# Where the keys and values of a second attention are projected: two other stages take them over

## The reference

```
x = x + decay_attention(layernorm(x))                       # L0_attn
x = x + causal_attention(layernorm(x), ctx, ctx)            # L0_xattn, bf16 projections
x = x + experts(layernorm(x))                               # L0_ffn: 8 experts, the best 2 for each token
x = x + rwkv_time_and_channel_mix(layernorm(x))             # L1_attn
x = x + biased_attention(layernorm(x), ctx, ctx, bias)      # L1_xattn
x = x + float8_ffn(x normalised)                            # L1_ffn
```

```
Q = query @ Wq.T + bq;  K = ctx @ Wk.T + bk;  V = ctx @ Wv.T + bv          # 16 heads of 16
scores = Q K^T / sqrt(16) + lambda_bias * bias ;  out = softmax(scores) V ;  out @ Wo.T + bo
```

## Time and profile before

| | us |
|---|---|
| median of 3 runs | 1992.35 (1987.86 to 1992.54) |
| profiled execution | 1993.02 |
| its span | 1991.2 |
| TensorE busy | 1691.7 (85%) |
| VectorE busy | 1248.1 (63%) |
| ScalarE busy | 1103.6 (55%) |
| GpSimd busy | 566.1 (28%) |
| granted TensorE clock, mean | 0.942 of full |

### The profile page before, as it was taken

One profiled execution on the slowest core, in us unless ns is written; L12 is line 12 of the kernel. 1 busy time (PEld: TensorE's weight loads), 2 busy tenths in 40 slices (PEclk: granted clock), 3 DMA queues, 4 the chain that ended last, 5 costly groups with the idle time before them and its releaser, 6 DMA issues. The chain is left out here.

```text
span 1991.2 us, 40593 instructions
## 1 busy us (share of the span) xinstructions
PE 1691.7 (85%) x13412; PEld 1393.7 (70%) x13412; DVE 1248.1 (63%) x4276; ACT 1103.6 (55%) x2520; POOL 566.1 (28%) x719
## 2 busy tenths in 40 slices
PE   6577777774899999999956999999988999999963
PEld 5455555553688888889944877787766888888842
DVE  6689999858211111111118999999936988888856
ACT  2299999920222222223325666666636888888845
POOL 3433233230211111101025566666520000000017
PEclk9899999976899999999977999999998999999975
DMA  3100010025455555558930000000001000000002
GB/s 117 47 26 25 19 26 18 2 80 183 135 180 187 181 186 183 185 174 267 323 129 14 19 22 22 22 22 22 12 12 40 23 23 23 23 23 23 2 1 85
DMA packets 102046, 154.64 MB, mean 78 GB/s; under 512 B 5760, under 2 KB 85504, under 8 KB 101088
## 3 DMA queue, kind: packets, MB, share of 16 engines
q1 hardware_dynamic: 85600, 125.25, 19.1%
q0 software_dynamic: 6480, 17.70, 3.0%
q10 hardware_dynamic: 9776, 9.31, 1.3%
HBM read 134.54 MB, written 17.69 MB: 76 GB/s over the span
## 5 line engine op out<-in xcount | busy, mean ns | idle before, releaser
L1836 ACT ACTIVATE moe_hT<-moe_p_h,lane_a 128x256 f32<-128x256 f32 (+1 forms) x344 | 131.4, 433 | 370.3 <-PE moe_p_h L1788 370.0
L1788 PE MATMUL moe_p_h<-moe_gT,moe_w 128*128 128x256 f32 (+1 forms) x1376 | 256.1, 345 | 0.8 <-issue 0.8
L1330 ACT ACTIVATE xb_pr<-xb_sc,xb_nmax 128x256 f32<-128x256 f32 x512 | 225.5, 502 | 50.7 <-DVE xb_nmax L1407 50.6
L1798 PE MATMUL moe_p_y<-moe_w,moe_hT 128*128 128x256 f32 x1136 | 252.3, 379 | 0.0
L1788 PEld LDWEIGHTS moe_p_h<-moe_gT,moe_w 128*128 128x128 f32 x1376 | 227.6, 192 | 25.7 <-issue 1.2
L1798 PEld LDWEIGHTS moe_p_y<-moe_w,moe_hT 128*128 128x128 f32 x1136 | 212.5, 190 | 27.1
L1407 DVE CUSTOM_DVE_ANT_0 xb_sc<-xb_p_s,xb_neg 128x256 f32<-128x256 f32 x512 | 187.0, 420 | 47.2 <-PE xb_p_s L1182 43.7
L837 ACT ACTIVATE xa_pr<-xa_sc,xa_nmax 128x256 f32<-128x256 f32 (+1 forms) x512 | 204.0, 453 | 17.6 <-DVE xa_nmax L917 17.2
L1705 POOL DMA_INDIRECT moe_gx<-moe_tokens,moe_source_i x71 | 67.4, 949 | 457.2 <-PE moe_p_t L1775 400.6
L1956 DVE COPY moe_gT<-moe_p_t 128x512 f32<-128x512 f32 (+1 forms) x43 | 25.7, 599 | 232.3 <-PE moe_p_t L1775 232.3
L1981 DVE TENSOR_TENSOR moe_gy<-moe_p_y,lane_a 128x256 f32<-128x256 f32 x71 | 27.5, 421 | 229.1 <-PE moe_p_y L1798 229.1
(11 more groups left out here) (331 smaller groups left out, 3454.3 us busy)
## 6 DMA issues: line engine op xcount, KB each, us to landing
moe_w<-in_L_ffn_w_dram SPq DMA_DIRECT2D x86, 1024.0 KB
moe_rows_out<-moe_gy ACTq DMA_DIRECT2D x28, 256.0 KB
X<-in_x_dram SPq DMA_DIRECT2D x4, 1024.0 KB, 10.9
xa_ctx<-in_ctx_turned_dram SPq DMA_DIRECT2D x16, 256.0 KB, 2.8
moe_tokens<-moe_XN_s SPq DMA_DIRECT2D x16, 256.0 KB, 2.1
xb_ctx<-in_ctx_turned_dram SPq DMA_DIRECT2D x16, 256.0 KB
xb_raw<-in_fside_BxSxS_dram SPq DMA_DIRECT2D x16, 256.0 KB
out_dram<-X SPq DMA_DIRECT2D x2, 1280.0 KB, 5.2
```

The costliest lines, as they stand in the source:

```text
L1330: last = act.activation(pr[:, n % RB, e, :], sc[:, n % RB, e, :], ACT.Exp, bias=nmax[:, n % RB, e:e + 1], scale=-1.0)
L1788: last = pe.matmul(p_h[n % 3][:, k * width:(k + 1) * width], w1[:, r, ic, (2 * n + k) * P:(2 * n + k + 1) * P], gT[:, r % 2, ic, 0:width], ...
L1798: last = pe.matmul(p_y[:, t * D:(t + 1) * D], hT[:, hc, t * P:(t + 1) * P], w2[:, r, hc, :], start=(hc == 0), stop=(hc == HC - 1))
L1836: last = act.activation(hT[:, 2 * n + k, 0:width], p_h[n % 3][:, k * width:(k + 1) * width], ACT.Gelu, bias=b1[:, bass.ds(e * HC + 2 * n + ...
```

## The change

Keys and values of the second attention are projected in `experts_ffn` (the first 18 units, `EARLY`) and in `time_channel_mix` (the other 14, `LATE`). Here a unit is one batch's keys or one batch's values: unit 2n is the keys of batch n, 2n+1 its values. They are stored to DRAM (`kv_all`) without their biases. `biased_attention` loads them, and GpSimd adds the biases.

In `experts_ffn` the weights and a ring of four contexts lie in slot 3 of the weights' ring and the results wait for their stores in slot 2, so the experts' weights for blocks 2 and 3 are loaded only when all stores have landed:

```diff
+            for u in range(3):
+                project_context(u)
             pe.wait_ge(s_["both_ready"], 1)
...
             pe.matmul(p_t[:, 0:NT * E], ones[:, :], both_v, start=True, stop=True).then_inc(s_["counted"], 1)
+            for u in range(3, 9):
+                project_context(u)
             for g in range(2 * NT // 8):
...
                 last.then_inc(s_["hot_read"], 1)
+                if g < 7:
+                    project_context(9 + g)
+            for u in range(16, EARLY):
+                project_context(u)
```

A unit is four products (`project_context`), into one of two new banks:

```diff
+            def project_context(u):
+                n, m = divmod(u, 2)
+                if u == 0:
+                    pe.wait_ge(s_["wkv_in"], 16)
+                if m == 0:
+                    pe.wait_ge(cx_in[n % 4], 16 * (n // 4) + 16)
+                if u >= 2:
+                    pe.wait_ge(s_["kv_read"], u - 1)
+                for k in range(DC):
+                    for ic in range(DC):
+                        if m == 0:
+                            last = pe.matmul(p_kv[m][:, k * S:(k + 1) * S], w_kv[:, 0, ic, k * P:(k + 1) * P], cx[:, n % 4, ic, :],
+                                             start=(ic == 0), stop=(ic == DC - 1))
...
+            def read_kv(u):
+                act.wait_ge(s_["kv_proj"], u + 1)
+                if u >= 8:
+                    act.wait_ge(kept_kv[u % 8], 16 * (u // 8))
+                act.activation(held[u % 8], p_kv[u % 2][:, :], ACT.Copy).then_inc(s_["kv_read"], 1)
```

ScalarE reads units 0 to 2 ahead of its two exponentials and the rest behind them. SP loads the weights at batch 6 of the first part and four contexts at batches 8 to 11, and then:

```diff
+            for u in range(4):
+                store_kv(u)
             sp.wait_ge(s_["owned"], 1)
             for j, r, i in groups(sp):
+                if isinstance(j, int) and j == 1:
+                    for u in range(4, 12):
+                        store_kv(u)
+                if isinstance(j, int) and j == 2:
+                    for u in range(12, EARLY):
+                        store_kv(u)
+                    for n in range(8):
+                        sp.wait_ge(kept_kv[n], 16 * ((EARLY - n + 7) // 8))
+                    sp.wait_ge(s_["kv_proj"], EARLY)
```

`store_kv(u)` waits for the read of unit u, and after an odd u it loads the context four further on. In `time_channel_mix` the same functions use `lane_a` for the weights, hid_sq for the contexts, hid for the results (a ring of four) and four banks:

```diff
+            for u in range(6):
+                project_context(u)
             turn_x(0, None)
+            project_context(6)
             for m in range(3):
                 project(0, m)
+            for u in range(7, 11):
+                project_context(u)
             pe.wait_ge(s_["xa_ready"], 1)
             turn_x(1, None)
+            for u in range(11, LATE):
+                project_context(u)
+            pe.wait_ge(s_["kv_read"], LATE)
```

In `biased_attention` the four functions of the keys and values go from TensorE's and VectorE's lists, GpSimd gets them, and the steps are ordered anew:

```diff
+            def finish_keys(n, h, s):
+                wait_alone(pool, s_["stood_p"], (kv_in[s], 32 * h + 32))
+                if since(n, 1):
+                    wait_alone(pool, s_["stood_p"], (s_["scored"], UNITS * (n - 1)))
+                for c in range(DC):
+                    last = pool.tensor_scalar(k[:, s, c, :], k_in[:, s, c, :], cols[:, 1, c:c + 1], None, ALU.add)
+                last.then_inc(s_["k_ready"], 1)
...
             for b, h, s in long_turns(pool, drain=2):
                 if since(b, 2):
                     add(b - 2)
+                if has_next(b):
+                    finish_keys(b + 1, h + s, 1 - s)
+                    finish_values(b + 1, 1 - s)
...
                 for g in range(STEPS if not at(b, B + 1) else 1):
+                    m = unit_before(b, g, 1)
+                    if m is not None:
+                        turn_unit(b, m)
+                        turn_unit(b, m + 1)
                     if runs(b):
                         scores(b, s, g)
...
-                    m = unit_before(b, g, 1)
                     if m is not None:
-                        turn_unit(b, m)
-                        turn_unit(b, m + 1)
+                        turn_unit(b, m + 2)
+                        turn_unit(b, m + 3)
                     if g == 0 and since(b, 2):
                         pe.wait_ge(s_["oT_ready"], b - 1)
                         project_rows(oT, 3, s_["y_ready"])
```

201 lines of the change are left out of this document (127 added, 74 removed).

## The result

The changed kernel takes 1969.26 us against 1992.44: ratio 0.9886, interval 0.9864 to 0.9907. The forecast was 1971. One of the four executions of the changed kernel took 3424.24 us, left no trace and is not in the ratio; the median of the other three is 1968.80. The profiled execution of the changed kernel took 1965.34 us with a span of 1963.2, the shortest of its runs, so the two profiles lie 28.0 us apart where the medians lie 23.2 apart.

What follows compares the result with a forecast made beforehand. TensorE sets the second attention's pace, with a chain through three engines nearly as long. Gains of 16.4 there, 2.0 in the experts' stage and 3.0 in the mixing stage sum to 21.4 us: 1971 us, range 1944 to 1989.

Steps and rivals of the forecast that it cites:

- The chain behind TensorE: Second attention: a chain through three engines is nearly as long as TensorE's work; a batch falls from 25.51 to 24.55 us.
- Step 1: Second attention, bare step: VectorE's copy wait of 1.47 us goes, ScalarE's exponentials and the turns set 5.5 us, was 5.71.
- Step 3: Second attention, step in which VectorE normalises between two shifts: VectorE's work sets 5.65 us, was 6.75.
- Step 0: Second attention: the turn of the sums meets VectorE's bias, ending at 5.53 us; 7.17 us in all, 0.35 worse.
- Step 2: Second attention: TensorE's work as before, 6.23 us; ScalarE's longest step, 7.0 us by estimate, spills into step 3.
- The ends: Second attention: batches 0 and 1 gain 1.6 us together, the last batch 0.6, the opening 1.7.
- GpSimd beside VectorE: Second attention: GpSimd's four additions take 2.6 us a batch and slow VectorE by 0, upper end 2.6 us a batch.
- Mixing stage: 14 units ahead of and beside its opening: first projections run at full clock, 3.0 us gained; bounds 5 gained, 18 lost.
- Experts' stage: 18 units in TensorE's idle time during routing: first block runs warm, 2.0 us gained; bounds 2.6 gained, 28 lost.
- Signs that did not come: Profile after: attention TensorE under 90%, ScalarE's exponentials releasing turns in steps 1 and 3, first expert block near 7.1 us.

Runs made afterwards that it cites:

- The removal alone: Changed kernel with the second attention's order of turns and copies taken back, keys and values still projected in the earlier stages: 1977.82 us, ratio 0.9918.
- the order alone: Kernel before with units m, m+1 turned ahead of the scores and copied first, keys and values still projected in the second attention: 1999.53 us, ratio 1.0034.
- the one with the rows first: Changed kernel with VectorE's scaling of the raw bias moved behind the first normalised rows at the second attention's opening: 1965.95 us, ratio 0.9854.
- steps of two orders put together: Changed kernel with the order of before in steps 0 and 2 of the second attention, new order in 1 and 3: 2015.53 us, ratio 1.0105.

## Why the prediction came out, step by step

- **The chain behind TensorE.** Right. The bare steps of the last batch foretold the old order without projections to 0.01 us, and the new order is what releases the rest: of 1.31 us a batch 0.49 comes from the removal and 0.82 from the order on top of it. The removal alone made the stage 8.5 us shorter, the order alone 10.5 us longer, both together 21.5 shorter.
- **Step 1**, forecast 5.5, was 5.06: the term that was mis-sized. I had charged the whole pair of turns (0.98 us) after ScalarE's second exponentials; unit m is turned while these run, and only the second turn (0.6) stands behind them. That ends at the same time as VectorE's loop, which sets the step.
- **Step 3**, forecast 5.65 by VectorE's way, was 5.70. **Step 0**, forecast 7.17, was 7.03, with the bias as releaser as forecast; the bias ended at 5.52 us into the step (forecast 5.53) and the turns behind it took 1.5 us to the next scores.
- **Two sums of the forecast don't come out of their terms.** Step 0 is 5.53 + 0.59 + 0.98 = 7.10 and not 7.17, and step 1 is 4.33 + 0.98 + 0.1 = 5.41 and not 5.5. With them a batch would have been 24.39 and the forecast about 1969.
- **Step 2**, forecast 6.23 as TensorE's unchanged work, was 6.41. The order is not free for TensorE: 0.15 us a step, seen with the order alone. The Trainium skill (TensorEngine Tiling (Array Packing), section "Key Properties") says that changing the tiling mode drains TensorE, and so speaks against an order with a fourth border; steps 2 and 3 of the runs agree with it by their 0.15 us, though none of them has the border alone. I had not weighed it. Right behind it comes ScalarE's copy of m+1, which held step 2 as soon as the turn of the rows was gone from it.
- **The ends.** Three steps of the last batch and the drain gave 3.6 us, forecast 0.6. The three steps gave 0.9, where their terms had said nothing or a little worse. From there to the last output projection it is 0.9 more: I had counted the last batch and not the two rounds of drain, which run the same chain. The other 1.8 are the clock in that projection, which no term of mine held. The opening gave 0 for 1.7: the raw bias now lands third, and VectorE scales it 4.9 us into the stage in place of 3.4.
- **GpSimd beside VectorE.** Right for the shifts, also with three times the additions. Not so at the opening: VectorE's normalised rows (two of 128x256, SBUF to SBUF) took 1.05 and 1.54 us there beside the additions, against 0.73 and 0.74 at the opening of the kernel before, with no addition beside them. The Trainium skill (SBUF — State Buffer, section "Who interferes with whom") lets such an operation contend with GpSimd in its modes with two ports; those rows agree. The four additions themselves take 3.26 us a batch, for the 2.6 that I had put down.
- **Mixing stage.** Right in sum and cause (3.0 us, the clock), shown by leaving the units out.
- **Experts' stage.** The routing was not delayed, but the first block did not run at full clock: I had taken the last two units as enough, and TensorE then stands 1.92 and 0.83 us before it. At most 1.0 us gained for 2.0.
- **Signs that did not come.** TensorE was to be under 90% busy in the attention and was at 93% of the batch shown. ScalarE's exponentials release a turn in step 1 (0.21 us), but in step 3 it is VectorE's copy (0.59). The first block was to take 7.1 us and took 8.83.
- **The 5 us by which the profiles lie further apart than the medians** are for the most part no effect of the change. Up to the routing the experts' stage took 46.02 us before and 42.11 after; the two other kernels with before's code there took 41.76 and 49.84. The granted clock rises at another time in each run, here in the kernel before, the changed one and the one with the rows first:
```profile
430.00:434.00 4.00, 4.00 (x17) 3.16 (x16) 1.94 (x8) 0.55 (x1) 1.47 (x3) 0.50 0.19 66
434.00:438.00 4.00, 4.00 (x17) 3.13 (x16) 1.78 (x7) 0.52 (x2) 0.85 (x3) 0.50 0.20 66
438.00:442.00 4.00, 4.00 (x28) 3.37 (x28) 2.11 (x9) 0.72 (x2) 1.16 (x3) 0.87 0.20 68
```
```profile
430.00:434.00 4.00, 4.00 (x23) 3.24 (x22) 2.14 (x9) 0.68 (x2) 1.78 (x3) 0.70 0.20 66
434.00:438.00 4.00, 3.93 (x32) 3.42 (x32) 3.39 (x14) 1.12 (x2) 1.85 (x4) 1.00 0.56 153
```
```profile
438.00:442.00 4.00, 4.00 (x18) 3.10 (x17) 1.71 (x8) 0.60 (x1) 0.89 (x2) 0.50 0.22 72
442.00:446.00 4.00, 4.00 (x25) 3.22 (x24) 2.06 (x9) 1.20 (x2) 1.16 (x3) 0.76 0.44 133
```

So near a hit was partly luck. In the profiles the attention gave 5.1 us more than forecast, 1.8 of them by the clock at its end, and the experts' hole 1.0 less. By the medians the gain is 23.2 us for a forecast of 21.4. Open is what the fourth border costs by itself, why the clock fell behind some of the waits and not behind others of the same length, and what sets the moment at which the clock rises in the gating part.

## What to carry to other kernels

Look for the one stretch of the trace in which the work to be removed is already missing (a last batch, a drain): it showed here what is late next in the old order, to the hundredth of a microsecond. For the new order it gave only the terms, and there the forecast missed one step by 0.4 us. When work is taken off the engine that sets the pace, reorder for the chain behind it, and read again after each move, since a wait that had just fitted comes up with the next row. A step's length belongs to the order that it was measured in: steps of two orders put together did not take the sum of their lengths, since work moved across the border between them. And leave an engine whose clock can fall no wait that you can fill: two waits of about 2 us a batch cost more than the order had won, even where the clock did not fall behind them.

## What the runs showed of the hardware

- With the same instructions and no waits, a step of TensorE with four borders between groups of different tile shape took 6.37 us and one with three 6.23. That the border costs the 0.14 us fits, and is not shown by itself.
- After 1.74 and 2.08 us of standing in the step, TensorE's next scores took 1.91 and 1.43 us in place of 1.15, and the granted clock was 0.66 over the next 5 us, part of them at 1.2 GHz. In the batch ahead the same waits were followed by none of this (granted clock 1.00, scores 1.15 us). After waits of 1.47 and 1.72 us in the old order it stayed at 2.4 GHz.
- The same gating code took from 41.8 to 49.8 us in fourteen profiles, by the moment at which the granted clock rose. That alone is 0.4% of this kernel's time.
- The last output projection of the attention took 1.99 us in five profiles and 3.38 to 3.78 in the nine others, by the granted clock there.
- VectorE's normalised rows (two of 128x256, SBUF to SBUF) took 1.05 and 1.54 us beside GpSimd's additions and 0.73 and 0.74 without; its shifts, which read PSUM, took at most 426 ns even with GpSimd busy 184 of 380 us.
